# Decoder kernel, self-attention layer: pair transpositions moved to odd slots and the small bank, opening order rewritten

## The chip, the cores and the metric

One core of one Trainium2 chip. The metric is the device time of one launch in microseconds (us), median over several executions of the same program. The core has five engines that run at once, each with its own list of instructions: TensorE (PE in the profile, PEld for its weight loads), VectorE (DVE), ScalarE (ACT), GpSimd (POOL) and SyncE (SP, which only issues DMAs here). Engines wait for each other through semaphores.

## The reference, cut to what matters

Sixteen sequences of 128 tokens with 128 features pass through three residual layers: causal self-attention without projections, cross-attention with a bias per head, and a decoder block with attention and a mixture of eight experts. The change touches the first of them and its opening.

```python
def _L0_attn_ref(x):                       # x: (16, 128, 128), already normalised
    q = k = v = x.reshape(B, S, 16, 8).transpose(0, 2, 1, 3)
    w = jnp.einsum('bhqd,bhkd->bhqk', q, k) / jnp.sqrt(8.)
    w = jnp.where(causal, w, mask_value)
    w = jax.nn.softmax(w, axis=-1)
    return jnp.einsum('bhqk,bhkd->bhqd', w, v).transpose(0, 2, 1, 3).reshape(B, S, D)
...
    x = x + _L0_attn_ref(_layernorm(x))
    x = x + _L0_xattn_ref(_layernorm(x), ctx_1024, bias, ...)
    x = x + _L0_ffn_ref(_layernorm(x), ...)
```

Queries, keys and values of the self layer are the same normalised rows. So what a batch needs is its normalised rows (values) and their transposition (keys, and queries after masking).

## The kernel before, in words

**Batches, slots, pairs.** The three layers give 48 attention steps, one batch of one layer each. Every engine runs a loop over slots `b` = 0 to 51 and in slot `b` does its share of step `b`, some of step `b - 1` and `b - 2`, and preparation for later steps. Slots 0 to 15 are the self layer, 16 to 31 the cross layer, 32 to 47 the attention of the last layer; behind them come the routing and 23 expert tiles. Two batches are a pair `q = b // 2`, and normalising and transposing are done for a pair at a time. The order on each engine is written out by hand; nothing is planned at run time, and each engine is strictly in its own order.

**Preparing a self pair.** DVE takes mean and variance (`norm_stats`, L991 and L995), POOL makes from them the inverse deviation and the shift (`inverse_deviation`, L374, L380, L385), ACT writes the normalised rows `xn` (`normalise`, L847), PE transposes both batches (`transposes`, recorded at L565, the helper `tr`), ACT copies the transposition to `kT` (`take_selfT`, L863), POOL multiplies it with the lane mask to `q_lane` (`self_queries`, L390), so that one matmul serves four heads, and POOL copies `xn` into the values `vaug` (`self_values`, L431). Before, the transpositions of pair `q + 3` stand at the end of even slot `b`, on all three engines in the same slot: ACT normalises behind the second exponential, PE transposes behind `add_outputs(b - 1)`, and POOL masks in slot `b + 1`.

**One self slot.** PE: the causal mask of the first half (two bf16 matmuls of `causal`), eight matmuls of scores (L562, `pair_banks<-q_lane,kT`), `out_transposed(b - 2)` into the small bank, and `add_outputs(b - 1)` (32 matmuls) into the work bank. ACT: `exponentials` of both halves (L880), then `take_out(b - 1)`, which copies the work bank to `outT` (L886). DVE: adds the causal mask to the second half of the scores in place (L1041), then `attention(b - 2)`: reciprocal (L1059), product `att` (L1065) and residual (L1070).

**Banks.** PSUM has three pairs of banks for scores, used in turn, and two single ones, `work` and `small`. `claim(name)` makes PE wait until the last reader of a bank has let it go. `work` holds `add_outputs` until `take_out` has read it, and before the change also the transpositions of every pair but pair 1. `small` holds `out_transposed` until `att` has been read.

Of the kernel before, what the change touches and what calls it, by code (L numbers as in the profile page):

```python
# [72 lines left out]
def build(nc, a, out):  # L73
# [4 lines left out]
    with ctx:  # L78
# [117 lines left out]
        s_qlane = sem("queries_masked")  # L196
        s_klane = sem("keys_masked")
# [51 lines left out]

        block = ctx.enter_context(nc.Block())  # L250
# [7 lines left out]
        def prep_bank(q):  # L258
            return small if q == 1 else work
# [108 lines left out]
        def _(pool):  # L368
# [108 lines left out]
            pool.wait_ge(s_lane, 4)  # L477
            self_queries(0)
            pool.wait_ge(s_dve_const, 1)
            self_values(0)  # L480
            inverse_deviation(2)
            self_queries(1)
            self_values(1)
            self_values(2)
# [23 lines left out]
            for b in range(LAST_SLOT):  # L508
                q = b // 2
                maxes = FIRST_CROSS <= b + 2 < FIRST_FFN  # L510
                if b == 0:
                    inverse_deviation(3)
                if b in LAST_NORMS:
                    inverse_deviation(NP + LAST_NORMS[b])
                if maxes:
                    subtract_maxes(b + 2, 0)
                if b % 2 == 0 and CROSS_PAIR <= q + 2 < NP:
                    masked_keys(q + 2)
                    if player(q + 2) == FFN:
                        masked_queries(q + 2)  # L520
                if b % 2 == 1 and q + 3 < NP:
                    if player(q + 3) == SELF:
                        self_queries(q + 3)
                    (self_values, cross_residuals, ffn_residuals)[player(q + 3)](q + 3)
                if b % 2 == 1 and q + 4 < NP:
                    inverse_deviation(q + 4)
                if maxes:
                    subtract_maxes(b + 2, 1)
                elif FIRST_FFN <= b + 2 < NB:
                    pool.wait_ge(s_dve_const, 3)  # L530
                    max_parts(b + 2)
                if b == 2:
                    constants()
                if b == 8:
                    pool.wait_ge(s_w, WEIGHTS)
                if b in LAST_NORMS:
                    rows_sum(LAST_NORMS[b])
# [22 lines left out]
        def _(pe):  # L560
# [12 lines left out]
            def transposes(q):  # L573
                bk = prep_bank(q)
                claim("small" if q == 1 else "work")
# [8 lines left out]
                if player(q) == SELF:  # L584
                    let_go["small" if q == 1 else "work"] = s_selfT, q + 1
                else:
                    let_go["work"] = s_hT, q - CROSS_PAIR + 1
# [47 lines left out]
            def self_scores(b):  # L635
# [4 lines left out]
                pe.wait_ge(s_qlane, b // 2 + 1)  # L640
# [15 lines left out]
            def ffn_scores(b):  # L656
                for half in range(2):
                    claim(PAIR_BANKS["exp", b, half])
                pe.wait_ge(s_qlane, CROSS_PAIR + b // 2 - FFN_PAIR + 1)
# [72 lines left out]
            for q in range(3):  # L732
                transposes(q)
# [3 lines left out]
            for b in range(LAST_SLOT):  # L737
# [4 lines left out]
                if b < FIRST_CROSS:  # L742
# [3 lines left out]
                    if b >= 1:  # L746
                        add_outputs(b - 1)
                    if values:
# [29 lines left out]
                if b % 2 == 0 and q + 3 < NP:  # L778
# [56 lines left out]
        def _(act):  # L835
# [24 lines left out]
            def take_selfT(q):  # L860
                act.wait_ge(s_t, q + 1)
                pair_done(act, q - NRING)
                nc.scalar.copy(kT[:, q % NRING, :], prep_bank(q)[:, 0:PAIR]).then_inc(s_selfT, 1)  # L863
# [40 lines left out]
            normalise(0)  # L904
            normalise(1)
            take_selfT(0)
            normalise(2)
            take_selfT(1)
            take_selfT(2)

            for b in range(LAST_SLOT):
# [5 lines left out]
                elif FIRST_CROSS <= b and b + NBIAS < FIRST_FFN:  # L917
                    load_bias(b + NBIAS)
                if b < FIRST_FFN:
                    exponentials(b, 1)  # L920
                    if b % 2 == 0:
# [13 lines left out]
                if b % 2 == 0 and q + 3 < NP:  # L935
                    if player(q + 3) == SELF:
                        take_selfT(q + 3)
                    else:
                        take_hT(q + 3)
# [33 lines left out]
        def _(dve):  # L973
# [117 lines left out]
            norm_stats(2)  # L1091

# [177 lines left out]
```

## Time and profile before

| | |
|---|---|
| time, three runs | 431.63, 429.36, 429.25 us; median 429.36 |
| span of the profiled execution | 431.3 us, first to last instruction |
| PE busy | 313.1 us, 73% of the span |
| POOL, DVE, ACT busy | 254.1, 249.6, 198.4 us |
| self layer's first scores, slots 0, 2, 10, 15 | 17.0, 29.7, 68.2, 102.4 us from the start |
| chain that ended last, by engine | PE 43%, issue 16%, POOL 15%, DVE 13%, ACT 8% |

The profiled execution is one of its own kind: its time isn't listed beside its span, and its span of 431.3 us lies 0.3 us below the longest of the three times and 1.9 us above their median. Busy time is the time in which an engine had an instruction running; matmuls overlap, and their ends are modelled. The chain is followed back from the last instruction, at each step to what released it.

### The profile page before, as it was taken

How to read it: one execution, taken by the hardware profiler on the slowest of the kernel's cores; microseconds unless marked ns; L12 is line 12 of the kernel's file. 1: busy time of each engine (PE TensorE's matmuls, PEld its weight loads, DVE VectorE, ACT ScalarE, POOL GpSimd, SP SyncE). 2: the span in 40 equal slices, each digit the busy share in tenths (PEclk: the TensorE clock that was granted, in tenths of full speed). 3: DMA queues.
4: the chain of work that ended last, by engine and by line, in shares of the span. 5: the costliest groups of instructions: out<-in, count | busy, mean ns of one | idle time of the engine just before them, and what ended most of it. 6: DMA issues, size and time to landing. Idle time of an engine off the chain costs nothing.

```text
span 431.3 us, 9910 instructions
## 1 busy us (share of the span) xinstructions
PE 313.1 (73%) x3435; PEld 203.1 (47%) x3435; DVE 249.6 (58%) x592; ACT 198.4 (46%) x390; POOL 254.1 (59%) x365
## 2 busy tenths in 40 slices
PE   1376888776779999989778788898875500199994
PEld 0133333432456666666544444444443400099893
DVE  5135454458999999997356455665622250067773
ACT  3347555544455565565344536456464200045451
POOL 5853343315889898999996638736340327324454
PEclk9969888999999999999899989999997555589998
DMA  6101443210358977921125990000000002323330
GB/s 165 31 2 56 123 117 110 74 38 14 97 156 184 219 191 162 212 27 22 12 26 136 283 297 24 2 2 2 2 2 2 1 24 108 95 53 103 93 90 18
DMA packets 67040, 36.36 MB, mean 84 GB/s; under 512 B 36253, under 2 KB 56864, under 8 KB 66992
## 3 DMA queue, kind: packets, MB, share of 16 engines
q1 hardware_dynamic: 57040, 15.79, 17.4%
q10 hardware_dynamic: 8448, 16.78, 13.7%
q0 software_dynamic: 1504, 3.16, 2.1%
q8 instruction: 29, 0.48, 0.5%
q14 instruction: 19, 0.16, 0.1%
HBM read 28.48 MB, written 7.69 MB: 84 GB/s over the span
## 4 chain that ended last, share of the span: by engine, by line
PE 43%; issue 16%; POOL 15%; DVE 13%; ACT 8%; DVEq 1%; DMA 1%; POOLq 0%; ACTq 0%; SPq 0%
PE pair_banks L562 23%; PE work_bank L562 9%; POOL biased L413 4%; DVE biased L1019 4%; ACT xn L847 4%; POOL routed_rows L545 3%; PE pair_banks L565 3%; PE work_bank L565 3%; PE small_bank L565 3%; PE small_bank L562 2%; POOL rstd L380 2%; DVE rowmax L1034 1%; ACT outT L886 1%; DVE att L1065 1%; POOL q_lane L390 1%
## 5 line engine op out<-in xcount | busy, mean ns | idle before, releaser
L880 ACT ACTIVATE probs<-pair_banks 128x1024 f32<-128x1024 f32 x96 | 97.5, 1023 | 68.6 <-PE pair_banks L565 36.0
L413 POOL TENSOR_TENSOR biased<-biased,rowmax 128x1024 f32<-128x1024 f32 x32 | 60.5, 1899 | 15.7 <-DVE rowmax L1026 15.5
L562 PE MATMUL work_bank<-probs,vaug 128*32 128x128 f32 x1536 | 53.6, 282 | 5.5 <-ACT hn2T L894 3.4
L562 PEld LDWEIGHTS work_bank<-probs,vaug 128*32 128x32 f32 x1536 | 40.3, 112 | 15.7 <-issue 8.6
L1041 DVE TENSOR_TENSOR pair_banks<-pair_banks,causal 128x1024 f32<-128x1024 f32 x16 | 19.7, 1233 | 47.7 <-PE pair_banks L562 47.7
L1034 DVE TENSOR_REDUCE rowmax<-pair_banks 128x8 f32<-128x1024 f32 x32 | 38.9, 1215 | 13.5 <-PE pair_banks L562 13.5
L374 POOL TENSOR_SCALAR vareps<-meanvar 128x2 f32<-128x2 f32 x32 | 7.4, 233 | 62.6 <-DVE meanvar L995 61.5
L562 PE MATMUL pair_banks<-q_lane,kT 32*128 32x512 f32 x256 | 42.3, 734 | 1.7 <-DVE biased L1019 1.7
L1019 DVE TENSOR_TENSOR biased<-pair_banks,bias_in 128x1024 f32<-128x1024 f32 x32 | 38.8, 1214 | 7.3 <-PE pair_banks L562 3.8
L552 POOL DMA_INDIRECT out<-vaug x23 | 22.6, 984 | 33.1 <-DVE vaug L1230 20.3
L562 PE MATMUL pair_banks<-k_lane,qT 32*128 32x512 f32 x256 | 37.5, 654 | 5.9 <-DVE biased L1019 4.0
L565 PE MATMUL work_bank<-ident,xn 128*128 128x128 f32 x46 | 11.0, 325 | 40.3 <-ACT xn L847 21.8
L1026 DVE TENSOR_REDUCE rowmax<-biased 128x8 f32<-128x1024 f32 x32 | 38.9, 1215 | 0.5
L565 PE MATMUL pair_banks<-ident,biased 128*128 128x128 f32 x256 | 35.7, 284 | 1.9
L565 PEld LDWEIGHTS pair_banks<-ident,biased 128*128 128x128 f32 x256 | 28.2, 143 | 18.3 <-issue 12.9
L390 POOL TENSOR_TENSOR k_lane<-kT,in_lane 128x1024 f32<-128x1024 f32 x16 | 30.3, 1895 | 0.3 <-ACT kT L870 0.3
L1215 DVE TENSOR_SCALAR probs<-pair_banks,b_cols 128x128 f32<-128x128 f32 x46 | 14.0, 346 | 27.8 <-PE pair_banks L562 27.3
L886 ACT COPY outT<-work_bank 128x256 f32<-128x256 f32 x48 | 17.6, 367 | 26.1 <-PE work_bank L562 26.0
L847 ACT ACTIVATE xn<-x_sb,shift,rstd 128x128 f32<-128x128 f32 x48 | 20.9, 484 | 14.5 <-POOL shift L385 14.5
L380 POOL TENSOR_TENSOR rstd<-vareps,minus_half 128x2 f32<-128x2 f32 (+1 forms) x32 | 25.6, 799 | 2.7
L565 PEld LDWEIGHTS work_bank<-ident,xn 128*128 128x128 f32 x46 | 5.0, 151 | 46.2 <-ACT outT L886 21.8
L562 PE MATMUL pair_banks<-xn,probs 128*128 128x128 f32 x184 | 26.1, 289 | 0.0
(143 smaller groups left out, 581.0 us busy)
## 6 DMA issues: line engine op xcount, KB each, us to landing
bias_in<-in_w SPq DMA_DIRECT2D x16, 256.0 KB, 7.3
routed_rows<-filler SPq DMA_DIRECT2D x2, 1028.0 KB, 9.1
vaug<-routed_rows SPq DMA_DIRECT2D x23, 64.5 KB
biased<-routed_rows SPq DMA_DIRECT2D x23, 64.0 KB
ctx_in<-in_ctx SPq DMA_DIRECT2D x8, 128.0 KB, 4.1
att_scratch<-att SPq DMA_DIRECT2D x16, 64.0 KB, 5.4
att_rows<-att_scratch SPq DMA_DIRECT2D x16, 64.0 KB, 2.9
routed_rows<-filler SPq DMA_DIRECT2D x1, 899.5 KB, 12.0
```

What stands on the lines that cost most here:

```text
L380: nc.gpsimd.tensor_tensor(rstd[:, i, 0:kinds, :].rearrange("p k s -> p (k s)"), vareps[:, 0:kinds, :].rearrange("p k s -> p (k s)"), minus ...
L390: return nc.gpsimd.tensor_tensor(dst, src.unsqueeze(1).to_broadcast([128, G, PAIR]), in_lane[:].unsqueeze(2).to_broadcast([128, G, PAIR]), ...
L413: nc.gpsimd.tensor_tensor(v, v, rowmax[:, b % 2, 8 * half:8 * half + 8].unsqueeze(2).to_broadcast([128, 8, S]), ALU.subtract).then_inc(s_s ...
L552: nc.gpsimd.indirect_dma_start(out=out.rearrange("b s d -> (b s) d"), out_offset=bass.IndirectOffsetOnAxis(ap=tile_res[:, buf, :].bitcast( ...
L562: return nc.tensor.matmul(o, lhsT, rhs, start=start, stop=stop, **kw)
L565: return nc.tensor.matmul(o, src, ident[:], start=True, stop=stop, is_transpose=True)
L847: last = nc.scalar.activation(dst, src, ACT.Identity, bias=shift[:, i, s:s + 1], scale=rstd[:, i, kind, s:s + 1])
L880: nc.scalar.activation(probs[:, b % 2, 2 * half:2 * half + 2, :], pair("exp", b, half), ACT.Exp, scale=1.0 if layer(b) == CROSS else SCALE ...
L886: nc.scalar.copy(outT[:, b % 2, :], work[:, 0:2 * S]).then_inc(s_out, 1)
L1019: nc.vector.tensor_tensor(biased[:, i, two, :], banks, bias_in[:, b % NBIAS, 8 * half:8 * half + 8, :].rearrange("p (g h) k -> p g (h k)", ...
L1026: nc.vector.tensor_reduce(peak, biased[:, i, two, :].rearrange("p g (h k) -> p (g h) k", k=S), AX.X, ALU.max).then_inc(s_rmax, 1)
L1034: nc.vector.tensor_reduce(peak, banks.rearrange("p g (h k) -> p (g h) k", k=S), AX.X, ALU.max).then_inc(s_mfree, 1)
```

## The change

1. The transposition of a self pair `q + 3` moves on PE from the end of even slot `b` to the end of the odd slot behind it (behind `add_outputs`), and goes to the small bank for pairs 1 and 3 to 7; pairs 0 and 2 keep the work bank. Cross and later pairs stay in even slots and in the work bank.
2. On ACT, `normalise(q + 3)` moves with it into the odd slot, between the two exponentials, and `take_selfT(q + 3)` stands behind the second exponential and ahead of `take_out`.
3. On POOL, `self_queries(q + 3)` stands behind `inverse_deviation(q + 4)` and no longer ahead of `self_values`.
4. The opening: PE transposes only pairs 0 and 1 ahead of slot 0, and pair 2 at the end of slot 0. ACT copies pair 0 right behind its normalisation and normalises pair 2 between the exponentials of slot 0. The first pair's queries are masked by DVE in two halves of 128 x 512 (`s_qfirst`), no longer by POOL. POOL does `self_values(0)` and `inverse_deviation(2)` in their place, and `inverse_deviation(3)` moves ahead of `self_values(2)`.

No operation is added or dropped but for the one masking that changes its engine and is split in two.

```diff
@@ -247,6 +248,8 @@
         WEIGHTS = 15 * 16
         MOE_LOADS = (2 * E + 2) * 16
 
+        banks_by_name = {"work": work, "small": small}
+
         block = ctx.enter_context(nc.Block())
 
         def tile_range(s, ahead):
@@ -256,7 +259,7 @@
             return q - NP if q >= NP else None
 
         def prep_bank(q):
-            return small if q == 1 else work
+            return "small" if q in (1, 3, 4, 5, 6, 7) else "work"
 
         def pair(kind, b, half):
             p = PAIR_BANKS[kind, b, half]
@@ -474,13 +477,13 @@
             nc.gpsimd.affine_select(out=causal[:], in_=causal[:], compare_op=ALU.is_ge, fill=MASKED, base=0,
                                     pattern=[[0, G], [1, S]], channel_multiplier=-1).then_inc(s_ident, 1)
             inverse_deviation(1)
-            pool.wait_ge(s_lane, 4)
-            self_queries(0)
             pool.wait_ge(s_dve_const, 1)
             self_values(0)
             inverse_deviation(2)
+            pool.wait_ge(s_lane, 4)
             self_queries(1)
             self_values(1)
+            inverse_deviation(3)
             self_values(2)
             self_queries(2)
             nc.gpsimd.memset(in_row[:], 0.0).then_inc(s_pool_const, 1)
@@ -508,8 +511,6 @@
             for b in range(LAST_SLOT):
                 q = b // 2
                 maxes = FIRST_CROSS <= b + 2 < FIRST_FFN
-                if b == 0:
-                    inverse_deviation(3)
                 if b in LAST_NORMS:
                     inverse_deviation(NP + LAST_NORMS[b])
                 if maxes:
@@ -519,11 +520,11 @@
                     if player(q + 2) == FFN:
                         masked_queries(q + 2)
                 if b % 2 == 1 and q + 3 < NP:
-                    if player(q + 3) == SELF:
-                        self_queries(q + 3)
                     (self_values, cross_residuals, ffn_residuals)[player(q + 3)](q + 3)
                 if b % 2 == 1 and q + 4 < NP:
                     inverse_deviation(q + 4)
+                if b % 2 == 1 and q + 3 < NP and player(q + 3) == SELF:
+                    self_queries(q + 3)
                 if maxes:
                     subtract_maxes(b + 2, 1)
                 elif FIRST_FFN <= b + 2 < NB:
@@ -571,8 +572,8 @@
                     pe.wait_ge(*let_go[bank])
 
             def transposes(q):
-                bk = prep_bank(q)
-                claim("small" if q == 1 else "work")
+                bk = banks_by_name[prep_bank(q)]
+                claim(prep_bank(q))
                 pe.wait_ge(s_xn, q + 1)
                 for s in range(2):
                     last = tr(bk[:, s * S:(s + 1) * S], xn[:, q % 2, s, :])
@@ -582,7 +583,7 @@
                         last = tr(bk[:, PAIR + s * S:PAIR + (s + 1) * S], ctx_in[:, q % 2, s, :])
                 last.then_inc(s_t, 1)
                 if player(q) == SELF:
-                    let_go["small" if q == 1 else "work"] = s_selfT, q + 1
+                    let_go[prep_bank(q)] = s_selfT, q + 1
                 else:
                     let_go["work"] = s_hT, q - CROSS_PAIR + 1
 
@@ -637,7 +638,10 @@
                 for g in range(2):
                     mm(bank_of("exp", b, g), identb[:], causal[:].rearrange("p g k -> p (g k)"), stop=False)
                 claim(PAIR_BANKS["exp", b, 1])
-                pe.wait_ge(s_qlane, b // 2 + 1)
+                if b < 2:
+                    pe.wait_ge(s_qfirst, b + 1)
+                else:
+                    pe.wait_ge(s_qlane, b // 2)
                 done = row_products("exp", b, kT, q_lane, start=None)
                 for half in range(2):
                     done[2 * half + 1].then_inc(s_e, 1)
@@ -656,7 +660,7 @@
             def ffn_scores(b):
                 for half in range(2):
                     claim(PAIR_BANKS["exp", b, half])
-                pe.wait_ge(s_qlane, CROSS_PAIR + b // 2 - FFN_PAIR + 1)
+                pe.wait_ge(s_qlane, CROSS_PAIR - 1 + b // 2 - FFN_PAIR + 1)
                 row_products("exp", b, kT, q_lane, start=True)
 
             def less_maxes(b):
@@ -729,8 +733,8 @@
                 let_go["small"] = s_res, b + 1
 
             pe.wait_ge(s_ident, 4)
-            for q in range(3):
-                transposes(q)
+            transposes(0)
+            transposes(1)
             pe.wait_ge(s_ident, 5)
             pe.wait_ge(s_dve_const, 2)
 
@@ -745,6 +749,10 @@
                         out_transposed(b - 2)
                     if b >= 1:
                         add_outputs(b - 1)
+                    if b == 0:
+                        transposes(2)
+                    if b % 2 == 1 and player(q + 3) == SELF:
+                        transposes(q + 3)
                     if values:
                         v_products(q + 2)
                 elif b < FIRST_FFN:
@@ -775,7 +783,7 @@
                     attention_transposed(c)
                 if b % 2 == 1 and CROSS_PAIR <= q + 3 < NP:
                     qk_products(q + 3)
-                if b % 2 == 0 and q + 3 < NP:
+                if b % 2 == 0 and CROSS_PAIR <= q + 3 < NP:
                     transposes(q + 3)
                 if c is not None:
                     out_projected(c)
@@ -860,7 +868,7 @@
             def take_selfT(q):
                 act.wait_ge(s_t, q + 1)
                 pair_done(act, q - NRING)
-                nc.scalar.copy(kT[:, q % NRING, :], prep_bank(q)[:, 0:PAIR]).then_inc(s_selfT, 1)
+                nc.scalar.copy(kT[:, q % NRING, :], banks_by_name[prep_bank(q)][:, 0:PAIR]).then_inc(s_selfT, 1)
 
             def take_qk(q):
                 first = 0 if player(q) == CROSS else 2
@@ -902,11 +910,9 @@
                              a["bias"][b - B].rearrange("h q k -> q h k")).then_inc(s_bias[i], 16)
 
             normalise(0)
+            take_selfT(0)
             normalise(1)
-            take_selfT(0)
-            normalise(2)
             take_selfT(1)
-            take_selfT(2)
 
             for b in range(LAST_SLOT):
                 q, c = b // 2, projected_first(b)
@@ -916,9 +922,17 @@
                     load_bias(BIAS_AT[b])
                 elif FIRST_CROSS <= b and b + NBIAS < FIRST_FFN:
                     load_bias(b + NBIAS)
+                if b == 0:
+                    normalise(2)
+                if b % 2 == 1 and player(q + 3) == SELF:
+                    normalise(q + 3)
                 if b < FIRST_FFN:
                     exponentials(b, 1)
-                    if b % 2 == 0:
+                    if b == 0:
+                        take_selfT(2)
+                    if b % 2 == 1 and player(q + 3) == SELF:
+                        take_selfT(q + 3)
+                    if b % 2 == 0 and player(q + 3) != SELF:
                         normalise(q + 3)
                 if 0 <= b - 1 < NB:
                     take_out(b - 1)
@@ -932,11 +946,8 @@
                     exponentials(b, 0)
                 if b % 2 == 1 and CROSS_PAIR <= q + 3 < NP:
                     take_qk(q + 3)
-                if b % 2 == 0 and q + 3 < NP:
-                    if player(q + 3) == SELF:
-                        take_selfT(q + 3)
-                    else:
-                        take_hT(q + 3)
+                if b % 2 == 0 and CROSS_PAIR <= q + 3 < NP:
+                    take_hT(q + 3)
                 if FIRST_FFN <= b < NB:
                     exponentials(b, 1)
                 if projected_second(b) is not None:
@@ -1089,6 +1100,12 @@
             nc.vector.tensor_copy(identb[:], ident[:]).then_inc(s_dve_const, 1)
             norm_stats(1)
             norm_stats(2)
+            dve.wait_ge(s_lane, 4)
+            dve.wait_ge(s_selfT, 1)
+            for n in range(2):
+                cut = slice(n * S, (n + 1) * S)
+                nc.vector.tensor_tensor(q_lane[:, 0, :, cut], kT[:, 0, cut].unsqueeze(1).to_broadcast([128, G, S]),
+                                        in_lane[:].unsqueeze(2).to_broadcast([128, G, S]), ALU.mult).then_inc(s_qfirst, 1)
 
             for b in range(LAST_SLOT):
                 q = b // 2
```

## Rows read from the trace of the kernel before

**Rows 1.** The page: busy tenths and granted clock in 40 equal slices.

```profile
PE   1376888776779999989778788898875500199994
...
PEclk9969888999999999999899989999997555589998
```

**Rows 2.** Chain that ended last, slot 4: start, length, what.

```profile
41.60 0.87 ACT xn L847 x2
42.47 0.27 ACT outT L886
...
42.78 0.69 PE work_bank L565 x2
```

**Rows 3.** Timeline, slots 2 to 4: start, length, engine, operation, [idle before].

```profile
34.32 0.44 PE L565 MATMUL work_bank<-ident,xn 128*128 128x128 f32 x2 [2.15 <-ACT outT L886]
...
35.12 1.14 PE L562 MATMUL pair_banks<-q_lane,kT 32*128 32x512 f32 x8
...
36.20 0.44 PE L565 MATMUL small_bank<-ident,outT 128*128 128x128 f32 x2
36.30 1.03 ACT L880 ACTIVATE probs<-pair_banks 128x1024 f32<-128x1024 f32 x1 [1.13 <-PE pair_banks L562]
36.43 1.23 DVE L1041 TENSOR_TENSOR pair_banks<-pair_banks,causal 128x1024 f32<-128x1024 f32 x1 [3.43 <-PE pair_banks L562]
36.56 1.08 PE L562 MATMUL work_bank<-probs,vaug 128*32 128x128 f32 x32
...
37.85 0.29 DVE L1065 TENSOR_TENSOR att<-small_bank,rowsum_inv 128x128 f32<-128x128 f32 x1
38.11 1.14 PE L562 MATMUL pair_banks<-q_lane,kT 32*128 32x512 f32 x8
...
40.68 1.02 ACT L880 ACTIVATE probs<-pair_banks 128x1024 f32<-128x1024 f32 x1 [0.37 <-PE work_bank L562]
```

**Rows 4.** Timeline, the opening, slots 0 to 2.

```profile
7.84 0.66 PE L565 MATMUL work_bank<-ident,xn 128*128 128x128 f32 x2 [7.84 <-ACT xn L847]
...
9.14 0.88 ACT L847 ACTIVATE xn<-x_sb,shift,rstd 128x128 f32<-128x128 f32 x2 [1.45 <-POOL shift L385]
...
10.07 0.69 PE L565 MATMUL small_bank<-ident,xn 128*128 128x128 f32 x2 [1.57 <-ACT xn L847]
...
15.58 0.66 PE L565 MATMUL work_bank<-ident,xn 128*128 128x128 f32 x2 [4.82 <-ACT xn L847]
15.77 1.89 POOL L390 TENSOR_TENSOR q_lane<-kT,in_lane 128x1024 f32<-128x1024 f32 x1 [1.25 <-ACT kT L863]
...
17.02 2.03 PE L562 MATMUL pair_banks<-q_lane,kT 32*128 32x512 f32 x8
...
19.10 1.02 ACT L880 ACTIVATE probs<-pair_banks 128x1024 f32<-128x1024 f32 x1 [2.45 <-PE pair_banks L562]
...
25.23 2.09 PE L562 MATMUL pair_banks<-q_lane,kT 32*128 32x512 f32 x8
...
27.25 1.94 PE L562 MATMUL work_bank<-probs,vaug 128*32 128x128 f32 x32
...
29.66 1.14 PE L562 MATMUL pair_banks<-q_lane,kT 32*128 32x512 f32 x8
```

**Rows 5.** Windows: busy of PE, PEld, DVE, ACT, POOL; granted clock, DMA share, GB/s.

```profile
42.78:46.00 3.22, 3.22 (x12) 1.09 (x12) 0.00 (x0) 0.37 (x1) 2.04 (x2) 0.50 0.65 181
...
110.00:150.00 40.00, 34.24 (x391) 23.98 (x390) 37.66 (x58) 21.10 (x41) 35.12 (x35) 1.00 0.69 174
```

**Rows 6.** Timeline: scores of slots 5, 10 and 11, and out_transposed of slot 5.

```profile
44.26 2.07 PE L562 MATMUL pair_banks<-q_lane,kT 32*128 32x512 f32 x8
...
46.25 0.44 PE L565 MATMUL small_bank<-ident,outT 128*128 128x128 f32 x2
...
68.24 1.14 PE L562 MATMUL pair_banks<-q_lane,kT 32*128 32x512 f32 x8
...
74.30 2.09 PE L562 MATMUL pair_banks<-q_lane,kT 32*128 32x512 f32 x8
```

More of the change, by code:

```diff
@@ L196, in build @@
         s_qlane = sem("queries_masked")
+        s_qfirst = sem("first_queries_masked")
         s_klane = sem("keys_masked")
```

## The prediction

> **What bounds the kernel now.** I read the page first: in the first quarter of the span PE is busy 1 to 8 tenths, in the cross layer that follows 9 tenths, and the granted clock is not full there either [rows 1]. So the self layer is not at the limit of any engine, and what it loses is waiting. The chain of waits says on what: in slot 4 it goes through ACT's normalisation of pair 5 (0.87 us), then `take_out`, and only then to PE's transpositions at 42.78 [rows 2]. The timeline shows the same gap on PE: the transpositions at 34.32 stand behind 2.15 us of idle time, released by `outT` [rows 3]. The reason is in the order: `add_outputs` has just filled the work bank, the transpositions claim the same bank, and the copy that frees it is queued on ACT behind the second exponential and the normalisation. The windows give the second half of the loss: behind such a gap PE ran at a granted clock of 0.50, the 1.2 GHz level [rows 5], and the next scores took 2.07 to 2.09 us in place of 1.14 [rows 3, 6]. Slots 5, 7, 9 and 11 all look so (5 and 11 are shown); slot 3, behind the gap of slot 2, does not. From scores(2) at 29.66 to scores(10) at 68.24 four pairs of slots take 38.58 us, 9.65 each [rows 4, 6].
>
> **The moved transpositions, slots 2 to 9.** I follow PE through one pair of slots with distances of start times at 2.4 GHz, all [rows 3].
> - Even slot. Scores to `add_outputs` 36.56 - 35.12 = 1.44; `add_outputs` to the next scores, with no transposition between, 38.11 - 36.56 = 1.55. Sum 2.99. The scores must also find the bank of the previous first exponential free, which ends 1.18 + 1.03 = 2.21 behind the scores: early enough.
> - Odd slot. `add_outputs` ends at 1.44 + 1.08 = 2.52. The transposition now waits for two others. The small bank is free when `att` is done: 37.85 + 0.29 - 35.12 = 3.02. `xn` is ready after the first exponential and the normalisation: 1.18, plus 0.92 from one to the other (40.68 to 41.60 in rows 2 and 3), plus 0.87, is 2.97. So PE waits 0.5 us where it waited 2.15, and starts at about 3.06. From transposition to next scores 35.12 - 34.32 = 0.80. Sum 3.86.
> - Together 6.85 us a pair of slots.
>
> What is late next? ACT. In the odd slot the second exponential now stands behind the normalisation and starts at about 2.9 (before, the mask on DVE set 1.31 + 1.23 = 2.54), then come `kT` and `take_out`, done at about 4.5. The next `out_transposed` wants that copy at 3.86 + 1.08 = 4.94. In the even slot the second exponential starts 2.57 behind the scores (38.11 to 40.68), `take_out` ends 1.3 later, 7.7 from the pair's start, and is wanted at 6.85 + 1.08 = 7.93. The cover is 0.2 to 0.4 us, thin. If it is gone, PE waits that much in front of `out_transposed` and no engine gains by it. For this and for handoffs I take 7.0 a pair. DVE and POOL have room: in 7.0 us DVE's mask of 1.23 comes twice [rows 3] and POOL's masking of 1.89 once [rows 4], and neither engine gets more work than it had in 9.65. The normalised rows are wanted a slot later than before, so the shift is ready earlier relative to its use; `self_queries` is used four slots later, so moving it behind `inverse_deviation` costs nothing. The queue of SP isn't touched. On ACT the bias DMAs keep their slots and lie in the wait for DVE's mask.
> Four pairs: 38.58 - 4 x 7.0 = **10.6 us**, with 11.2 at 6.85 and 8.6 at 7.5 (the latter if PE pays 0.65 per pair for late ACT copies).
>
> **The opening.** All [rows 4], at the slow level as the rows have it there.
> - The transposition of pair 1 stays at 10.07, since the shift that releases `xn` at 9.14 isn't moved. Behind it come now the causal matmuls and the scores: 17.02 - 15.58 = 1.44 after a transposition, so scores(0) at 11.51.
> - DVE's masking: the transposition of pair 0 ends at 7.84 + 0.66 = 8.50, and its copy, of the size of `outT` at 0.27 in the chain [rows 2], now goes ahead of the second normalisation and ends at about 8.95. No row shows this multiplication on DVE. From below the 128-wide product's 0.29 us, from above half of POOL's 1.89, or 0.95; the mask addition on DVE, 1.23 for 1024 columns [rows 3], is the nearest in kind and gives 0.62 a half. I take that: halves ready at 9.6 and 10.2, at worst at 9.9 and 10.9. Both are ahead of 11.51. So this edit hides in the whole range and costs nothing; `norm_stats(3)`, queued behind it, is wanted at 20.
> - The first exponential follows 2.08 behind the scores (17.02 to 19.10), at 13.59; the normalisation of pair 2 0.92 later, 14.51 to 15.39; its transposition at 15.44, scores(1) 1.44 later at 16.88, against 25.23: 8.3 us earlier. Here PE waits in its own order for ACT with 1.9 us idle, since scores(1) itself would have been ready to run; that is the price of the transposition of pair 2 in slot 0.
> - `add_outputs(0)` 27.25 - 25.23 = 2.02 later, at 18.90, 1.94 long, to 20.84. The normalisation of pair 3 ends 2.1 + 0.92 + 0.87 behind scores(1), at 20.8. Transposition at 20.85, scores(2) 0.80 (fast) to 1.44 (slow) later: 21.65 to 22.3, I take 22.0 against 29.66: **7.7 us**. If the slow level lasts a slot more, it is 2 us less: the bound of this part is 5.7 to 8.0.
>
> POOL's masking of pair 1 isn't wanted before scores(2), and POOL, which starts it once the second copy is there at about 11.2 and takes 1.89, has it done long before.
>
> **Slots 10 and later** keep their order: pair 8 is a cross pair in the even slot with the work bank. The step of 6.06 us from scores(10) to scores(11), with a gap and the slow level [rows 6], stays; I take nothing for it, and up to 1.5 us if the clock stays high. The cross layer is paced by DVE, 37.66 us busy in 40 [rows 5], and starts when it is reached. Its first bias is issued in slot 4 and read in slot 14, so no data are late there.
>
> **Sum.** scores(10) at 22.0 + 28.0 = 50.0, against 68.24: 18.2 us. The profiled execution would fall from a span of 431.3 to 413.1; it lies 1.9 us above the median run, and against that median I forecast 429.36 - 18.2 = **411.2 us**.
>
> **A rule that speaks against it.** Between 110 and 150 us PE ran at granted clock 1.00 with a share busy of 34.24 in 40, in a stretch in which many matmuls are transpositions [rows 5]. The Trainium skill, "TensorE: Matmul & The Clock Gate", in "Part 1: The HAM clock gate", says that the throttled state is the default and activity releases it, and in "Part 4: PE-mode transpose" that transpositions do not count as activity in the same way. By the rule the new self slots, in which transpositions fill the place of idle time, could stay slow; that would be rival 3 below. The row from 110 on agrees with the first section and bears the second out badly.
>
> **Rivals.**
> 1. The clock still falls once per pair. For: the gaps before did this in four of five cases. Against: the gap of slot 2 wasn't followed by it, and the gap shrinks from 2.15 to 0.5 us. Price: scores 0.95 more, `add_outputs` 0.86 more, some 0.45 for transposition and causal matmuls, 2.3 a pair; four pairs 9.2. Time 420.4.
> 2. The gain is given back later: the cross layer starts 18 us sooner and waits for a transfer. For: DMA share 0.69 in it already [rows 5]. Against: the bias is issued by slots, ten ahead at first, and DVE is the pace. It would have to lose over half: 421 or more.
> 3. **Slower:** PE stays at 1.2 GHz from slot 2 to slot 12. A slow slot is scores to `out_transposed` 46.25 - 44.26 = 1.99 [rows 6], to `add_outputs` about 0.65, 1.94 for these, and 1.0 or 1.44 to the next scores: 5.6 even and 6.0 odd, 11.6 a pair, 46.4 in place of 38.58. With the opening's 5.7 gained and 4 us lost in slots 10 to 12, which run fast in part before, it is 429.4 + 7.8 - 5.7 + 4 = 435.5. It decides from a period of 10.1 us on ((38.58 + 5.7 - 4) / 4). Against it: PE has work in 6.3 of 6.85 us, more than from 110 on, where the clock is full.
> 4. The gap of slot 10 isn't followed by the slow level any more: 1.5 us more, 409.7.
>
> **How the numbers follow.** Forecast 0.68, rival 4 0.16, rival 1 0.09, rival 2 0.04, rival 3 0.03. The low end: 411.2 - 0.6 (period 6.85) - 0.3 (opening) - 1.5 (rival 4) - 1.3 for phases of the clock elsewhere = 407.5. The high end: + 2.0 (period 7.5) + 2.0 (opening) + 1.8 for a slow slot somewhere = 417.0. This leaves rivals 1 to 3 out, 0.16. The three runs of before span 2.4 us, so I call under 1% (4.3 us) no change; faster by over 1% is all but rival 3 and a part of rival 2: 0.95, within 1% 0.02, slower 0.03.
>
> **What would show it.** Scores(0), (1), (2) at 11.5, 16.9 and 22.0, and scores(10) at 50. PE's transpositions L565 from `xn` in slots 3, 5, 7, 9 with some 0.5 us idle ahead of them, released by `att` or `xn`, not by `outT`. Scores of the self layer at 1.14 us from slot 2 to 10, with granted clock 1.00. DVE's two masks ending before 11. From scores(10) on every distance as before. The prediction is wrong if 2.0 us scores return in odd slots, if ACT's copy `outT` delays `out_transposed` by more than 0.5 us, or if the distance from scores(10) to the last instruction grows.

## The result and the profile after

The changed kernel takes 414.15 us (median of four runs, 413.54 to 415.12) against 429.31 us for the kernel before in the same comparison: 15.2 us less, ratio 0.9613 with a 95% interval of 0.9567 to 0.9658. Forecast were 411.2 us, 18.2 us less. All ratios leave out executions that took over 1.5% more than the shortest of the same kernel, so a ratio isn't always the quotient of the two medians beside it.

The profiled executions lie further apart than the medians: spans of 431.3 and 412.2 us, 19.1 us. For the execution after, both numbers are on record, a time of 414.06 us for the span of 412.2, so some 1.9 us lie around a span. By that the profiled execution of before took about 433.2 us and was a long one of its kind.

The page after, beside [rows 1]. The first quarter of the span now has PE at 6 to 9 tenths from the second slice on:

```profile
PE   0899867669899999896888798888785400199993
...
PEclk9999989987999999998999899999998555589999
```

The opening in the timeline after, beside [rows 4]: start, length, engine, operation, [idle before].

```profile
9.00 1.39 DVE L1107 TENSOR_TENSOR q_lane<-kT,in_lane 128x512 f32<-128x512 f32 x2 [0.52 <-ACT kT L871]
9.03 1.51 POOL L434 COPY vaug<-xn 128x128 f32<-128x128 f32 x2
...
10.05 0.69 PE L566 MATMUL small_bank<-ident,xn 128*128 128x128 f32 x2 [1.56 <-ACT xn L855]
...
11.53 2.09 PE L563 MATMUL pair_banks<-q_lane,kT 32*128 32x512 f32 x8
...
14.57 0.87 ACT L855 ACTIVATE xn<-x_sb,shift,rstd 128x128 f32<-128x128 f32 x2
...
15.58 0.66 PE L566 MATMUL work_bank<-ident,xn 128*128 128x128 f32 x2 [1.96 <-ACT xn L855]
...
17.03 2.09 PE L563 MATMUL pair_banks<-q_lane,kT 32*128 32x512 f32 x8
...
21.08 0.66 PE L566 MATMUL small_bank<-ident,xn 128*128 128x128 f32 x2
...
22.29 1.14 PE L563 MATMUL pair_banks<-q_lane,kT 32*128 32x512 f32 x8
```

Scores(0), (1) and (2) start at 11.53, 17.03 and 22.29 us, where they stood at 17.02, 25.23 and 29.66 [rows 4]. So the opening gives 7.37 us.

One odd slot and what follows it, in the timeline after, beside [rows 3]:

```profile
25.27 1.14 PE L563 MATMUL pair_banks<-q_lane,kT 32*128 32x512 f32 x8
...
26.45 1.02 ACT L888 ACTIVATE probs<-pair_banks 128x1024 f32<-128x1024 f32 x1 [0.30 <-PE pair_banks L563]
...
27.37 0.87 ACT L855 ACTIVATE xn<-x_sb,shift,rstd 128x128 f32<-128x128 f32 x2
...
28.00 0.29 DVE L1076 TENSOR_TENSOR att<-small_bank,rowsum_inv 128x128 f32<-128x128 f32 x1
28.14 1.01 ACT L888 ACTIVATE probs<-pair_banks 128x1024 f32<-128x1024 f32 x1
...
28.38 0.41 PE L566 MATMUL small_bank<-ident,xn 128*128 128x128 f32 x2 [0.59 <-DVE att L1076]
...
29.15 1.14 PE L563 MATMUL pair_banks<-q_lane,kT 32*128 32x512 f32 x8
...
32.14 1.14 PE L563 MATMUL pair_banks<-q_lane,kT 32*128 32x512 f32 x8
...
35.59 0.44 PE L566 MATMUL small_bank<-ident,xn 128*128 128x128 f32 x2 [0.93 <-DVE att L1076]
```

The reader is to see three things. The transposition starts 3.1 us behind the scores, when `att` is done (28.29 us; `xn` is done at 28.24), and waits no longer for `outT`; the second exponential stands behind the normalisation; and the scores behind the gap take 1.14 us. The odd slot takes 3.88 us, the even slot 2.99 (forecast 3.86 and 2.99). In slots 5 and 9 the wait is 0.93 and 1.19 us.

The windows of slots 2 to 9 and of slots 10 to 14 after (columns as in [rows 5]):

```profile
22.29:50.76 28.47, 25.17 (x362) 12.52 (x361) 21.73 (x57) 22.35 (x40) 15.88 (x34) 1.00 0.40 113
50.76:84.82 34.06, 24.15 (x266) 12.01 (x265) 18.64 (x39) 17.60 (x32) 13.82 (x21) 0.95 0.27 74
```

Four pairs of slots take 28.47 us in place of 38.58 [rows 4, 6], 10.1 us less, at granted clock 1.00. From scores(10) to scores(15) the distance is 34.06, before 34.18. So scores(15) come 17.6 us earlier; up to the routing (342.72 and 325.28 us in the two traces) this has become 17.4, and the rest to 19.1 arises behind it, mostly expert tiles, which the change doesn't touch.

### The profile page after: what moved, and what is told of

Its sections match the earlier page's. It is cut to its first block, busy times and chain, and to the rows that moved or that the text cites. A ratio compares the mean times of both kernels' runs of the same rounds, so it can differ in the third digit from the quotient of the medians.

```text
span 412.2 us, 9912 instructions
## 1 busy us (share of the span) xinstructions
PE 309.1 (75%) x3435; PEld 203.1 (49%) x3435; DVE 251.4 (61%) x594; ACT 197.4 (48%) x390; POOL 253.0 (61%) x364
## 3 DMA queue, kind: packets, MB, share of 16 engines
q1 hardware_dynamic: 57040, 15.79, 18.2%
## 4 chain that ended last, share of the span: by engine, by line
PE 44%; DVE 14%; issue 12%; POOL 9%; ACT 7%; DMA 1%; POOLq 0%; DVEq 0%; ACTq 0%
PE pair_banks L563 25%; PE work_bank L563 8%; DVE biased L1030 5%; PE pair_banks L566 4%; POOL routed_rows L546 4%; PE work_bank L566 3%; ACT xn L855 3%; POOL biased L416 2%; PE small_bank L566 2%; PE small_bank L563 2%; DVE rowmax L1045 1%; DVE att L1076 1%; ACT outT L894 1%; DVE pair_banks L1052 1%; DVE rowmax L1037 1%
## 5 line engine op out<-in xcount | busy, mean ns | idle before, releaser
L563 PE MATMUL pair_banks<-k_lane,qT 32*128 32x512 f32 x256 | 38.8, 677 | 4.3 <-DVE biased L1030 2.2
L563 PE MATMUL pair_banks<-q_lane,kT 32*128 32x512 f32 x256 | 39.3, 686 | 1.7 <-DVE biased L1030 1.7
L566 PEld LDWEIGHTS pair_banks<-ident,biased 128*128 128x128 f32 x256 | 29.5, 148 | 18.7 <-issue 13.6
L566 PE MATMUL pair_banks<-ident,biased 128*128 128x128 f32 x256 | 37.0, 291 | 1.7
L566 PE MATMUL work_bank<-ident,biased 128*128 128x128 f32 x12 | 3.5, 295 | 30.3 <-DMA biased<-routed_rows 30.3
L566 PE MATMUL work_bank<-ident,xn 128*128 128x128 f32 x36 | 8.2, 311 | 24.0 <-ACT xn L855 14.2
L546 POOL DMA_INDIRECT routed_rows<-rows_out,position_i x16 | 15.7, 979 | 17.0 <-DVE tile_expert_i L1214 12.4
```

What stands on the lines that cost most here:

```text
L546: nc.gpsimd.indirect_dma_start(out=routed, out_offset=bass.IndirectOffsetOnAxis(ap=position_i[:, n:n + 1], axis=0), in_=rows_out[:, n, :], ...
L563: return nc.tensor.matmul(o, lhsT, rhs, start=start, stop=stop, **kw)
L566: return nc.tensor.matmul(o, src, ident[:], start=True, stop=stop, is_transpose=True)
```

## The experiments

**Each part alone.** Two kernels: one has the new opening and the old slots, the other the old opening and pairs 4 to 7 in the new place. The opening alone, against the changed kernel (ACT and POOL follow):

```diff
-            return "small" if q in (1, 3, 4, 5, 6, 7) else "work"
+            return "small" if q in (1, 3) else "work"
-                    if b % 2 == 1 and player(q + 3) == SELF:
+                    if b == 1:
                         transposes(q + 3)
...
-                if b % 2 == 0 and CROSS_PAIR <= q + 3 < NP:
+                if b % 2 == 0 and b >= 2 and q + 3 < NP:
                     transposes(q + 3)
```

The slots alone, against the kernel before (pairs 4 to 7 leave the even slots, and ACT and POOL follow):

```diff
-            return small if q == 1 else work
+            return "small" if q in (1, 4, 5, 6, 7) else "work"
+                    if b >= 3 and b % 2 == 1 and player(q + 3) == SELF:
+                        transposes(q + 3)
```

> The changed kernel with its opening alone (pairs 0 to 3 as changed, pair 3 in slot 1); pairs 4 to 7 are transposed again at the end of even slots 2 to 8, in the work bank. Theory, two gains that add: scores(2) stays at 22.3 us as in the changed kernel, and from there the distances of the kernel before come back (38.6 us to scores(10), with the gap of 2.15 us), so that 7.4 us of the gain are left: 421.9 us. Rival, the earlier start is given back, because PE reaches the same waits at another phase of its clock: 425 us or more.

> The kernel before with only pairs 4 to 7 moved to odd slots and the small bank; opening and pair 3 as before. Theory: scores(2) at 29.7 us as before, then four pairs of slots in 28.5 us in place of 38.6, so 10.1 us less at scores(10): 419.2 us. Rival, the two parts need each other, since the slow clock of the opening reaches into slot 3: a gain under 7 us, 422.5 us or more.

Measured: the opening alone 426.5 us against 432.19, ratio 0.9832 (0.9767 to 0.9898); the slots alone 422.4 us, ratio 0.9775 (0.972 to 0.983). The times expected for these two runs and the next two (421.9, 419.2, 427.8 and 423.3 us) were counted from 429.3 us for the kernel before. In this comparison it took 432.19, 2.9 us more, and the four measured times lie 4.6, 3.2, 2.4 and 3.2 us above the expected ones. So the times don't decide between the expectations here; the traces do. The timeline of the first shows slots 2 to 4, that of the second slots 7 to 10:

```profile
21.85 1.14 PE L565 MATMUL pair_banks<-q_lane,kT 32*128 32x512 f32 x8
26.53 0.69 PE L568 MATMUL work_bank<-ident,xn 128*128 128x128 f32 x2 [2.15 <-ACT outT L896]
28.00 2.01 PE L565 MATMUL pair_banks<-q_lane,kT 32*128 32x512 f32 x8
31.85 1.14 PE L565 MATMUL pair_banks<-q_lane,kT 32*128 32x512 f32 x8
```

```profile
50.26 0.41 PE L569 MATMUL small_bank<-ident,xn 128*128 128x128 f32 x2 [0.59 <-DVE att L1075]
51.03 1.14 PE L566 MATMUL pair_banks<-q_lane,kT 32*128 32x512 f32 x8
54.02 1.14 PE L566 MATMUL pair_banks<-q_lane,kT 32*128 32x512 f32 x8
57.74 0.44 PE L569 MATMUL small_bank<-ident,xn 128*128 128x128 f32 x2 [1.20 <-DVE att L1075]
58.54 1.14 PE L566 MATMUL pair_banks<-q_lane,kT 32*128 32x512 f32 x8
```

At scores(15) the opening alone is 6.5 us ahead of the kernel before (95.92 against 102.42), the slots alone 10.0 us (92.39), together 17.6. The gains add, with 1.1 us on top. The opening alone is 7.8 us ahead at scores(2), and gives 1.5 back in slot 3, whose scores now take 2.01 us behind the same gap that was harmless in the trace of before. So the rival of a gain given back is true for a fifth of it, in a trace in which the gap is still there. The slots alone take 28.47 us for the four pairs, to the hundredth what they take in the changed kernel.

**The bank alone**, against the kernel before.

```diff
-            return small if q == 1 else work
+            return "small" if q in (1, 3, 4, 5, 6, 7) else "work"
```

> The kernel before with its order kept on every engine; pairs 3 to 7 are only transposed into the small bank. Theory, the order on ACT sets the wait: PE now waits for the normalisation behind the second exponential in place of the copy behind that, 0.3 us less a pair, five pairs, and the clock still falls: 427.8 us, gap at least 1.8 us. Rival, the shared bank was the cause: the gap shrinks to 0.6 us as in the changed kernel, and with the clock kept it is 419 to 422 us.

Measured: 430.24 us against 432.19, ratio 1.0006 (0.9965 to 1.0047), no difference; in the trace scores(15) come 1.6 us earlier (100.82). The gap stays, here in slot 6:

```profile
52.12 0.41 PE L567 MATMUL small_bank<-ident,xn 128*128 128x128 f32 x2 [1.98 <-ACT xn L849]
```

It shrinks by 0.17 us only and is now released by `xn` in place of `outT`. The shared bank alone was not the limit: with it gone, PE waits for the input that stands in ACT's queue. The rival is out.

**ACT's order alone taken back**, against the changed kernel.

```diff
-                if b % 2 == 1 and player(q + 3) == SELF:
-                    normalise(q + 3)
                 if b < FIRST_FFN:
                     exponentials(b, 1)
...
                     if b % 2 == 1 and player(q + 3) == SELF:
+                        normalise(q + 3)
                         take_selfT(q + 3)
```

> The changed kernel with one thing put back: in odd slots ACT normalises behind both exponentials, not between them; bank and slot of the transpositions stay. Theory, the place on ACT is what the move lives on: xn is ready 4.4 us behind the scores in place of 3.0, PE's gap in odd slots grows from 0.6 to about 1.9 us, each pair of slots takes 1.3 us more, and where the clock falls behind that gap another 1.5: scores(10) at 56 to 62 us in place of 50.8, time 420 to 426 us. Rival, the slot and the bank are enough, and the gap stays under 1 us: time the same as the changed kernel.

Measured: 423.84 us against 432.34, ratio 0.9839 (0.9775 to 0.9902); scores(10) at 61.24, in the upper part of what was expected. Its timeline, slots 3 and 4:

```profile
30.33 1.02 ACT L888 ACTIVATE probs<-pair_banks 128x1024 f32<-128x1024 f32 x1 [0.37 <-PE work_bank L563]
...
31.25 0.87 ACT L855 ACTIVATE xn<-x_sb,shift,rstd 128x128 f32<-128x128 f32 x2
...
32.26 0.41 PE L566 MATMUL small_bank<-ident,xn 128*128 128x128 f32 x2 [1.98 <-ACT xn L855]
...
33.03 1.89 PE L563 MATMUL pair_banks<-q_lane,kT 32*128 32x512 f32 x8
```

With new slot and new bank, but the normalisation behind the second exponential, the gap is 1.98 us again and the slow clock is back, though not behind every gap: scores(4), (6), (8) and (10) take 1.89, 1.49, 1.14 and 2.09 us. From scores(2) to scores(10) it is 61.24 - 23.38 = 37.9 us, which leaves 0.7 us of the 10.1. So in this trace the new slot and bank without the new place of the normalisation gain next to nothing. That the odd slot and the small bank are needed to let it stand there is argued from the order; the early normalisation with the old slot or the old bank wasn't run.

**The gap filled, not removed.** The kernel before gets eight matmuls whose results are overwritten, ahead of each transposition of slots 0 to 10; in a second version it gets twelve transpositions of the identity.

```diff
+                if b % 2 == 0 and b <= 10:
+                    claim(PAIR_BANKS["exp", b + 1, 0])
+                    for n in range(8):
+                        mm(bank_of("exp", b + 1, n % 2), identb[:], causal[:].rearrange("p g k -> p (g k)"))
                 if b % 2 == 0 and q + 3 < NP:
                     transposes(q + 3)
...
+                    for n in range(12):
+                        tr(bank_of("exp", b + 1, n // 4 % 2)[:, n % 4 * S:(n % 4 + 1) * S], ident[:])
```

> The kernel before with eight more matmuls of the causal mask (into the bank that the next slot's scores overwrite anyway) in each gap ahead of the transpositions of slots 0 to 10: PE is kept busy some 1.8 us there, and nothing else changes. Theory, half of the slots' gain is the clock and not the wait: scores of slots 5, 7, 9 and 11 take 1.14 us in place of 2.09, slots 5, 7 and 9 each save some 1.5 us with what is around them, slot 11 about 1.3, in all 6 us: 423.3 us. Rival, the slow level comes from something else than PE's idle time: no gain, 429 to 430 us.

> As the run with filled gaps (kernel before, PE kept busy ahead of the transpositions of slots 0 to 10), but the filling is twelve 128x128 transpositions of the identity in place of matmuls. Theory, transpositions keep the clock as matmuls do: scores of slots 5, 7 and 9 at 1.14 us and 33.8 us from scores(2) to scores(10). Rival, by the Trainium skill (TensorE: Matmul & The Clock Gate, Part 4: PE-mode transpose) transpositions do not count as activity in the same way: scores of slots 5, 7 and 9 at 2.09 us as before, 38.6 us from scores(2) to scores(10).

Measured: matmuls 426.49 us against 432.19, ratio 0.9844 (0.9784 to 0.9905); transpositions 427.43 us against 432.34, ratio 0.9885 (0.9817 to 0.9954). The second version has two executions only. The two timelines, slots 4 and 5 (seven of the eight matmuls are in the trace):

```profile
38.32 1.67 PE L562 MATMUL pair_banks<-causal,identb 128*128 128x512 bf16 x7 [0.16 <-issue]
40.31 0.44 PE L565 MATMUL work_bank<-ident,xn 128*128 128x128 f32 x2 [0.32 <-ACT outT L890]
40.58 0.59 PE L562 MATMUL pair_banks<-causal,identb 128*128 128x512 bf16 x2
41.11 1.14 PE L562 MATMUL pair_banks<-q_lane,kT 32*128 32x512 f32 x8
```

```profile
39.65 1.53 PE L565 MATMUL pair_banks<-ident 128*128 128x128 f32 x12
41.87 0.44 PE L565 MATMUL work_bank<-ident,xn 128*128 128x128 f32 x2 [0.69 <-ACT outT L890]
42.14 0.59 PE L562 MATMUL pair_banks<-causal,identb 128*128 128x512 bf16 x2
42.67 1.14 PE L562 MATMUL pair_banks<-q_lane,kT 32*128 32x512 f32 x8
```

The transposition stands as far behind the scores as before (40.31 - 35.64 = 4.67 us, before 42.78 - 38.11 = 4.67), and yet PE does more work in less time: 33.84 us from scores(2) to scores(10) with matmuls and 33.83 with transpositions, in place of 38.58. The granted clock over this stretch is 1.00 in both, and 0.87 before. A pair takes 33.84 / 4 = 8.46 us, and the one pair of slots that had the full clock before, slots 2 and 3, took 38.11 - 29.66 = 8.45. So 4.74 us were the clock alone. The Trainium skill ("TensorE: Matmul & The Clock Gate", "Part 4: PE-mode transpose") lets one expect that transpositions do not hold the clock; here they do, with the same 1.14 us scores behind them. Other matmuls stand on both sides of them, so whether transpositions alone would raise the clock isn't shown.

**The DVE mask.** Against the changed kernel, POOL masks again; the masking on DVE and its semaphore are gone.

```diff
             inverse_deviation(1)
+            pool.wait_ge(s_lane, 4)
+            self_queries(0)
             pool.wait_ge(s_dve_const, 1)
             self_values(0)
```

> The changed kernel with the first pair's queries masked by POOL again, ahead of the first pair's values, as before; the rest of the new opening stays. Theory, the masking on DVE is worth nothing: POOL would end it at about 11.0 us, scores(0) starts at 11.5 either way, and the shift of pair 2 comes at 13.5 to 14.0, ahead of the 14.6 at which ACT normalises: scores(1) at 17.0, scores(2) at 22.3, time the same within 0.5 us. Rival, the DVE mask is a needed part of the opening, because the shift of pair 2 comes late: scores(1) 1 us or more later.

Measured: 414.34 us, against 415.68 for the changed kernel in the same comparison and 430.49 for the one before (ratios 0.9625, 0.9566 to 0.9683, and 0.962, 0.9565 to 0.9676). Scores(1) stand at 17.03, as with the DVE mask. POOL's timeline, and PE in slots 10 and 11:

```profile
9.05 1.89 POOL L393 TENSOR_TENSOR q_lane<-kT,in_lane 128x1024 f32<-128x1024 f32 x1
10.90 0.52 POOL L434 COPY vaug<-xn 128x128 f32<-128x128 f32 x2
...
12.64 0.50 POOL L388 TENSOR_SCALAR shift<-meanvar,rstd 128x1 f32<-128x1 f32 x2
...
54.99 0.44 PE L567 MATMUL work_bank<-ident,xn 128*128 128x128 f32 x2 [2.15 <-ACT outT L892]
...
56.01 1.14 PE L564 MATMUL pair_banks<-q_lane,kT 32*128 32x512 f32 x8
```

The shift is ready at 13.1, 1.5 us before ACT wants it at 14.57. That edit of the change brings nothing. PE's lines show something else: the gap of slot 10 is 2.15 us as ever, and scores(11) behind it take 1.14 us, where they took 2.09 in the traces of before and after. From scores(10) to scores(12) this trace needs 61.41 - 50.32 = 11.09 us, the one after 12.30. So the slow clock doesn't follow such a gap each time. In all traces there are 24 gaps of 1.87 to 2.15 us ahead of a transposition in slots 2 to 10; behind 19 of them the scores took longer than 1.14 us. Behind the 26 gaps of 0.58 to 1.20 us, in the kernels with moved transpositions, none did.

**Further.** Pair 8, the first cross pair, gets the same treatment; then DVE's constants move out of slots 4 and 8 as well. Pair 8, against the changed kernel:

```diff
-            return "small" if q in (1, 3, 4, 5, 6, 7) else "work"
+            return "small" if q in (1, 3, 4, 5, 6, 7, 8) else "work"
-                if b % 2 == 1 and player(q + 3) == SELF:
+                if b % 2 == 1 and player(q + 3) == SELF or b == 10:
                     normalise(q + 3)
...
+                    if b == 10:
+                        take_hT(q + 3)
```

The constants, against that: the five memsets of slot 4 move as they are behind `norm_stats(3)` of slot 0; the wait for the weights and the scaling of `cols` and `w_xq` move from slot 8 to slot 1, `row_lane` and `pick` from slot 8 to slot 11.

```diff
                 if b == 0:
                     norm_stats(3)
+                    nc.vector.memset(maxparts[:], 0.0).then_inc(s_dve_const, 1)
...
-                if b == 8:
+                if b == 11:
```

> The changed kernel as it is, once more, so that the next three have it on their own chip. All theories expect what it gave: scores(2) at 22.3, scores(10) at 50.8, scores(15) at 84.8 us in the trace, and a time 14 to 17 us under the kernel before.

> The changed kernel, and pair 8 (the first cross pair, slot 10) treated likewise: its transpositions in the small bank, its normalisation between the two exponentials of slot 10, its copy ahead of the copy of the outputs. Theory: the last gap of 2.15 us falls to about 0.8 us and scores(11) takes 1.14 in place of 2.09, so scores(11) comes 1.8 us and scores(12) 3 us earlier, 411 us. Rival, slots 11 to 15 are set by ACT and DVE and take the gain back: scores(15) less than 1 us earlier.

> The kernel of the run before this, and DVE's constants of slots 4 and 8 (five memsets; four small steps) moved to slot 0, slot 1 and slot 11. Theory: in slots 5 and 9 PE waits 0.93 and 1.19 us for the product of the attention, in slots 3 and 7 0.59, and the difference is these constants ahead of DVE's mask; all four at 0.59 gives 0.36 + 0.65, 1.0 us less at scores(10), 49.8 us. Rival, the longer waits come from elsewhere (ACT's order): no difference at scores(10).

Measured, all against 430.49 us for the kernel before: the changed kernel again 415.68 us, ratio 0.962 (0.9565 to 0.9676); with pair 8 412.34 us, ratio 0.9546 (0.9483 to 0.9609); with the constants too 408.92 us, ratio 0.9468 (0.9415 to 0.952). The last timeline, slots 9 to 11:

```profile
48.55 0.41 PE L566 MATMUL small_bank<-ident,xn 128*128 128x128 f32 x2 [0.59 <-DVE att L1078]
49.32 1.14 PE L563 MATMUL pair_banks<-q_lane,kT 32*128 32x512 f32 x8
52.43 0.41 PE L566 MATMUL small_bank<-ident,xn 128*128 128x128 f32 x2 [0.58 <-DVE att L1078]
53.42 1.14 PE L563 MATMUL pair_banks<-q_lane,kT 32*128 32x512 f32 x8
```

With pair 8, scores(10) to scores(12) take 58.68 - 49.19 = 9.49 us in place of 63.06 - 50.76 = 12.30: 2.8 us. By the trace with POOL's mask (11.09) some 1.2 us of it is clock and 1.6 the shorter wait (0.59 in place of 2.15 us). Up to scores(15) 1.9 us of it are left in this trace, and all 2.8 in the next one. With the constants out of the way all gaps of slots 3 to 10 are 0.58 or 0.59, and scores(2) to scores(10) take 49.32 - 21.86 = 27.46 us, 1.0 less than 28.47, as expected, though scores(10) don't stand at the expected 49.8 but at 49.32: scores(2) came 0.4 us earlier than in the first trace of the changed kernel, as they also did in its second (21.88). By its median this is the fastest version.

## Why the prediction was right, and where it was not

- **What bounds.** Right: the wait for `outT` behind the normalisation, and the slow clock behind it. The split can now be given. Of the 10.1 us in slots 2 to 9, 4.7 are clock (filled gaps) and 5.3 are waits: four gaps of 2.15 us are 8.60, and 0.59 + 0.93 + 0.59 + 1.19 are 3.30.
- **The moved transpositions.** 7.0 us a pair of slots were forecast; measured are 28.47 / 4 = 7.12, and 6.87 with the constants of DVE removed. The allowance of 0.15 over 6.85 was put down to thin cover on ACT; it was DVE's constants in slots 4 and 8, which the walk through the order had left out. Each stands ahead of a mask that `att` waits for. They don't do it alone: the residual ahead of them takes 0.94 us there in place of 0.29 (last section). Without these 0.65 us the masks at 33.86 and 48.20 would have started 1.31 us behind their scores (32.14 and 46.24), as in an undisturbed slot. This is an estimate from the rows; only the constants were moved in a run. The cover on ACT held.
- **The opening.** 7.7 us forecast, 7.37 found; each of the steps lies within 0.3 us of its forecast. DVE's mask was put at 0.62 us a half and took 0.70, hidden as said. The copy ahead of it was read from the chain as 0.27 us, which is the time to the next link; the copy itself took 0.37, and this moved nothing. That the edit is worth nothing follows from the run with POOL's mask.
- **Slots 10 to 15.** Unchanged, as said: 34.06 against 34.18 us.
- **The sum.** scores(10) at 50.76, forecast 50.0. Of the 18.2 us forecast there, the traces show 17.5; the medians show 15.2. The step that failed is the last, the subtraction: "it lies 1.9 us above the median run, and against that median I forecast". The 1.9 us compared a span with a time. With what lies around a span the profiled execution was 3.8 us above the median of the runs shown, and a gain read from a long execution was taken off short ones. The kernel before run again gave medians of 430.49, 432.19 and 432.34 us; the 22 executions that count for the ratios took from 426.41 to 433.37 us. They show what goes with it: the five shortest (up to 429.74 us) had mean granted clocks of 0.916 to 0.922, the ten longest (from 431.3 us) 0.898 to 0.911. The profiled one of before had 0.906. So the prediction took its gain from an execution with more slow clock than the short ones, and took it off the short ones. Behind scores(15), where nothing was changed, the twelve traces take from 325.8 to 330.9 us, enough to hold the missing 2 to 3 us; in which stage the short executions of before save them wasn't profiled and stays open. Two traces of the changed kernel differ by 0.41 us at scores(2), where the last transpositions took 0.66 us in one and 0.44 in the other, and by 2.3 in the span (granted clocks 0.920 and 0.908). The range had no term for all this. That 414.15 us lies inside it (407.5 to 417.0) is in this part luck: the room at its high end was meant for slow slots and late copies that didn't come.
- **Rivals.** The clock that still falls once a pair did not happen in slots 2 to 9 of the changed kernel, but the late normalisation brings much of it back. Nothing was given back to a transfer. The rule on transpositions, on which the slower rival leaned, did not hold in the run made for it. The high clock in slot 11 did not come in the two traces of the changed kernel (scores(11) took 2.09 us), but it came by itself in the trace with POOL's mask. So what this rival says happens in some executions; with pair 8's gap gone, both traces have it.

## What to carry to other kernels

A gap on TensorE can cost twice: the wait itself, and what runs behind it at the slow clock (here behind 19 of 24 gaps of about 2 us). Fill the gap with matmuls that nobody reads, and the second half can be measured by itself before anything is reordered. When a claimed bank seems to be the wait, look at the queue of the engine that is to free it: another bank alone gave nothing here, since the input of the step stood in the same queue. And subtract like from like: a span from a span, or a median from a median. Look at the mean granted clock of the profiled execution before taking it for a typical one.

## What was not expected of the hardware

Where DVE multiplied or added two SBUF operands while POOL worked, one of the two, or both, took longer. Timeline after, slots 4 and 5:

```profile
30.45 1.23 DVE L1052 TENSOR_TENSOR pair_banks<-pair_banks,causal 128x1024 f32<-128x1024 f32 x1 [1.04 <-PE pair_banks L563]
...
31.11 1.90 POOL L393 TENSOR_TENSOR q_lane<-kT,in_lane 128x1024 f32<-128x1024 f32 x1
...
32.20 0.94 DVE L1081 TENSOR_TENSOR x_sb<-x_sb,att 128x128 f32<-128x128 f32 x1
...
33.86 1.20 DVE L1052 TENSOR_TENSOR pair_banks<-pair_banks,causal 128x1024 f32<-128x1024 f32 x1
```

The residual on DVE takes 0.29 us alone and 0.94 here, and ends 0.13 us behind POOL's masking (33.14 and 33.01), which keeps its 1.90 us. In the opening, POOL's two copies took 1.51 us beside DVE's mask and 0.52 without it. In both cases the one that started second took longer; whether DVE's mask was also held up isn't shown, since it never ran without the copies. Where the two started within 0.03 us of each other (28.33 and 28.30), the residual took 0.41 us and the two copies 0.59, both more than alone. The mask addition of 1.23 us, with an operand in PSUM, kept its length beside POOL. The Trainium skill ("GPSIMD Engine Reference", "1. Specifications", under SBUF interfaces) says that they are shared with VectorE, with contention where a DVE instruction has two SBUF inputs; these rows agree with it. The new order on POOL put its masking beside this residual; with the constants gone the residual still takes 0.94 us and PE's wait is 0.59, so it costs nothing there.
